# Cross-attention block: column-quartered matmuls gathered into one group in two steps

## The reference

```python
x = layer_norm(hidden_states, ln1_w, ln1_b)
q = (x @ q_w + q_b)          # 16 heads of 32
k = (ctx @ k_w + k_b); v = (ctx @ v_w + v_b)
attn = softmax(where(mask, q k^T * scale, min))
out = (attn @ v) @ cproj_w + cproj_b
hidden = out + hidden_states
y = gelu(layer_norm(hidden, ln2_w, ln2_b) @ fc_w + fc_b) @ proj_w + proj_b
return hidden + y
```

## Time and profile before

| | |
|---|---|
| median of 3 runs | 826.39 us (824.57 to 826.96) |
| the profiled execution | 823.19 us, span 821.4 us |
| TensorE matmuls busy | 788.1 us (96%) |
| VectorE busy | 449.1 us (55%) |
| GpSimd busy | 314.6 us (38%) |
| ScalarE busy | 276.6 us (34%) |

### The profile page before, as it was taken

How to read it: one execution, slowest core, us unless ns; L and a number is a source line. 1 busy time by engine, 2 the same in 40 slices (tenths; PEclk the granted TensorE clock), 3 DMA queues, 4 the chain that set the end, 5 groups by cost and what they waited for, 6 DMA issues and landing times.

```text
span 821.4 us, 9736 instructions
## 1 busy us (share of the span) xinstructions
PE 788.1 (96%) x3728; PEld 558.1 (68%) x3728; DVE 449.1 (55%) x711; ACT 276.6 (34%) x483; POOL 314.6 (38%) x190
## 2 busy tenths in 40 slices
PE   7899999999999998999898899999999999999998
PEld 5788888644445444544543688888888888888886
DVE  6853344787866897688789735633323332332122
ACT  4434241366654654467347101121112111111111
POOL 2724040166973875488648436432002110112000
PEclk9999999999999999999999999999999999999999
DMA  8476385836534533537331245004000400020001
GB/s 308 129 243 231 120 253 143 257 79 161 125 91 131 166 79 91 168 79 182 102 103 39 69 150 162 31 0 155 1 0 1 154 1 0 1 84 20 0 1 51
DMA packets 53102, 85.39 MB, mean 104 GB/s; under 512 B 5344, under 2 KB 13796, under 8 KB 53056
## 3 DMA queue, kind: packets, MB, share of 16 engines
q1 hardware_dynamic: 52912, 84.75, 34.8%
q10 hardware_dynamic: 144, 0.02, 0.0%
HBM read 59.45 MB, written 25.18 MB: 103 GB/s over the span
## 4 chain that ended last, share of the span: by engine, by line
PE 79%; DVE 14%; DMA 2%; issue 2%; ACT 1%; SPq 1%; POOL 0%; DVEq 0%; POOLq 0%
PE ps L383 20%; PE ps L384 20%; PE ps L385 20%; DVE mx L859 5%; PE ps L483 5%; PE ps L499 5%; PE ps L468 5%; PE ps L514 3%; DVE BIG L899 2%; DVE R L976 1%; PE ps L527 1%; DVE R L864 1%; DVE R L818 1%; DMA R<-in_k_w 1%; PE ps L442 1%
## 5 line engine op out<-in xcount | busy, mean ns | idle before, releaser
L1123 POOL TENSOR_TENSOR R<-Pt 128x1024 f32<-128x1024 f32 x59 | 144.1, 2460 | 127.3 <-PE ps L514 76.6
L859 DVE TENSOR_REDUCE mx<-ps 128x1 f32<-128x512 f32 x256 | 162.8, 680 | 40.7 <-PE ps L468 40.4
L692 ACT ACTIVATE Pt<-ps 128x512 f32<-128x512 f32 x256 | 135.0, 600 | 99.7 <-PE ps L483 96.5
L1012 DVE CAST HR<-R 128x512 fp32r<-128x512 f32 x52 | 24.2, 466 | 184.6 <-ACT R L726 184.6
L726 ACT ACTIVATE R<-ps,cols 128x512 f32<-128x512 f32 x52 | 35.9, 690 | 205.4 <-PE ps L385 205.4
L468 PE MATMUL ps<-BIG 97*128 97x512 f32 x256 | 94.6, 414 | 9.2 <-DVE mx L859 9.2
L483 PE MATMUL ps<-BIG 98*128 98x512 f32 x256 | 99.5, 433 | 3.6 <-ACT Pt L692 2.3
L483 PEld LDWEIGHTS ps<-BIG 98*128 98x128 f32 x256 | 43.9, 191 | 71.2 <-ACT Pt L692 36.8
L383 PE MATMUL ps<-BIG,HR 128*128 128x512 f32 x192 | 74.9, 390 | 2.7 <-DVE HR L1014 2.7
L383 PE MATMUL ps<-YT,BIG 128*128 128x512 f32 x192 | 75.8, 395 | 0.0
L385 PE MATMUL ps<-YT,BIG 128*128 128x512 f32 x192 | 74.8, 390 | 0.0
(11 more groups left out here) (107 smaller groups left out, 1298.0 us busy)
## 6 DMA issues: line engine op xcount, KB each, us to landing
BIG<-qs SPq DMA_DIRECT2D x48, 256.0 KB
BIG<-ks SPq DMA_DIRECT2D x48, 256.0 KB
ks<-BIG SPq DMA_DIRECT2D x32, 256.0 KB, 2.0
qs<-BIG SPq DMA_DIRECT2D x32, 256.0 KB, 5.5
R<-hd SPq DMA_DIRECT2D x28, 256.0 KB, 4.2
R<-in_x SPq DMA_DIRECT2D x16, 256.0 KB, 4.5
hd<-R SPq DMA_DIRECT2D x16, 256.0 KB, 2.0
RW<-in_fc_w SPq DMA_DIRECT2D x16, 256.0 KB, 2.8
```

The costliest lines, as they stand in the source:

```text
L692: eng.activation(Pt[:, r, j % 2, :], bank(3 + place % 3), ACT.Exp, scale=SCALE).then_inc(S["a_ra"], 1)
L859: eng.tensor_reduce(mx[:, s % 2, 4 * j + qc:4 * j + qc + 1], bank(place % 3), AX.X, ALU.max).then_inc(S["v_rb"], 1)
L1123: eng.tensor_tensor(R0[:, 2 * hp:2 * hp + 2, :], Pt[:, (r - 2) % 6, :, :], Pt[:, r, :, :], ALU.add).then_inc(S["g_ac"], 1)
```

## The change

The sums of a pair and the products of two steps now stand together, in one group in every second step: at an even step i, before `s2(i, 2)`, come the sums of steps i-4 and i-3, then `pv(i - 2)` and `pv(i - 1)`. The pair sums have a second place (half of RAWY to pair 17, then RW to pair 21; from there R0 alone again), so that GpSimd waits for an earlier sum. `divide_a` moves from m=1 to m=2 of its step. The first slabs' load also waits for the last sum that reads RW. In batch 0, the second x is turned behind the last Q projection, with ScalarE's and VectorE's parts of it.

```diff
+        SECOND = RW.rearrange("p a (h t) -> p (a h) t", h=2)
+        def pair(m):
+            if m % 2 == 0 or m > 21:
+                return R0[:, :, :]
+            return RAWY[:, 0] if m <= 17 else SECOND
+        def pair_before(m):
+            return m - 1 if m < 23 else m
...
                 if f < 2:
                     sp.wait_ge("p_pv", 48)
+                    sp.wait_ge("p_sm", 22)
...
-                    ins = eng.matmul(bank(7)[32 * j:32 * j + 32, :], ones[:, :], R0[:, j, :], start=kc == 1, stop=kc == 3)
+                    ins = eng.matmul(bank(7)[32 * j:32 * j + 32, :], ones[:, :], pair(i // 2)[:, j, :], start=kc == 1, stop=kc == 3)
...
+            def columns(i):
+                if i >= 4:
+                    sums((i - 4) // 4, (i - 4) % 4 + 1)
+                pv(i - 2)
+                pv(i - 1)
...
-                    if b == 0 and g == 1:
+                    if b == 0 and g == 3:
                         x_turn(1)
...
                 for m in range(4):
+                    if m == 2 and i >= 2 and i % 2 == 0:
+                        columns(i)
                     if m >= 2:
                         s2(i, m)
...
-                    if m == 2 and kc == 1 and i >= 5:
-                        sums(s - 1, 3)
...
-                if kc == 3:
-                    sums(s, 1)
-                if i >= 1:
-                    pv(i - 1)
...
-            pv(NI - 1)
+            columns(NI)
...
-                    if m == 1 and i >= 5 and kc == 2:
+                    if m == 2 and i >= 5 and kc == 2:
                         divide_a(s - 1)
...
-                    dve.wait_ge("p_sm", i // 2)
-                    eng.tensor_tensor(R0[:, 2:4, :], Pt[:, (r - 2) % 6, :, :], Pt[:, r, :, :], ALU.add).then_inc(S["v_ac"], 1)
+                    dve.wait_ge("p_sm", pair_before(i // 2))
+                    eng.tensor_tensor(pair(i // 2)[:, 2:4, :], Pt[:, (r - 2) % 6, :, :], Pt[:, r, :, :], ALU.add).then_inc(S["v_ac"], 1)
...
-                        else:
-                            pool.wait_ge("p_sm", i // 2)
-                        eng.tensor_tensor(R0[:, 2 * hp:2 * hp + 2, :], Pt[:, (r - 2) % 6, :, :], Pt[:, r, :, :],
+                        elif i >= 5:
+                            pool.wait_ge("p_sm", pair_before(i // 2))
+                        eng.tensor_tensor(pair(i // 2)[:, 2 * hp:2 * hp + 2, :], Pt[:, (r - 2) % 6, :, :], Pt[:, r, :, :],
```

## The result

The kernel with the change takes 862.3 us (median of 4, 858.46 to 863.76) against 826.16 us (4, 824.57 to 826.96) before: a ratio of 1.043, 95% interval 1.0395 to 1.047. It is slower, as forecast, but by 36 us and not by 12; the time lies 12 us above the end of the range. The profiled execution has a span of 860.7 us (before 821.4), with a mean granted clock of 0.968 (before 0.992): some 55 us of it at 1.2 GHz, against 13 before.

A forecast was written before the change was run, and what follows sets the result against it. It took TensorE (97% busy) as the bound, VectorE close behind and setting the new loops. Start +0.8, steps 4 to 20 +6.1, 20 to 36 +2.1, 36 to 52 +0.9, tail +1, turn +0.8: +11.7, so 838 us, range 823 to 850.

The forecast's parts named there:

- The two loops: Plain attention steps: loop without divides 7.0 us, with divides 9.1, or 9.7 with the wait for GpSimd.
- The lock: VectorE's last divide waits for GpSimd's pair add to end: 0.6 us, bounds 0 and 2.4, in eight loops.
- The start: Second x turned later in batch 0: TensorE's stall grows by 0.65 us; taken as +0.8, bounds -3 and +1.5.
- The fourth rival: TensorE's clock falls in the loops, a group costing up to 2.7 us more: 847 to 855 us; chance 0.11.
- the first: The rival in which the attention loops hold as worked out: slower, 829 to 845 us; chance 0.68.
- case 1: The likeliest outcome, attention loops as worked out and slower: 838 us; chance 0.68.
- ScalarE at nothing: Attention loops: the forecast's sum held no term for waits on ScalarE's exponentials.
- An even step's end at its own length: VectorE's work at an even step's end counts in full: 0.7 us a statistic, 0.6 the variances, 0.7 a turned y.
- The sum: Whole kernel: all terms together +11.7 us on the profiled execution's 823.19, giving 834.9, or 838 as median.

The follow-up runs named there:

- experiment 9: Changed kernel with three repeats of a first-pass matmul at m=2 of kc=3 and m=0 of kc=0, outside the projections' steps: 858.5 us, ratio 1.040.
- experiment 2: Changed kernel with VectorE's maxima reading 32 of 512 columns: 830.9 us, ratio 1.010 to the kernel before.
- experiment 4: Changed kernel with all three divides ahead of the maximum of m=2 at kc=2, where VectorE idles for the group: 835.4 us, ratio 1.014.
- Experiment 6: Kernel before with only the two places for the pair sums, no column group moved: 827.7 us, ratio 1.007.
- experiment 3: Changed kernel with one place for the pair sums, every pair in R0: 862.3 us, ratio 1.048 to the kernel before.
- experiment 8: Kernel before with the lone sums of kc=1 joined to that step's product, and the first divide ahead of the maximum of m=0 at kc=2: 824.7 us, ratio 1.003.

## Why the prediction was right in sign and short in size

**The two loops: right.** 7.24 for 7.0, and 9.61 for 9.7; VectorE's idle at a group 2.18 and 2.32 for 2.1. Four plain steps at full clock take 16.85 us, 1.5 more than before; experiment 9 held that at full clock (7.25 and 9.63), and experiments 2 and 4 show that it is the divides in VectorE's queue.

**The lock: right as a mechanism.** Experiment 6 shows it alone, experiment 3 its absence. The 0.6 us taken for a divide compare with 1.14 - 0.68 = 0.46 at the median. In two loops, at steps 31 (above) and 27, it was 2.2, inside the bounds; at twice 2.2 - 0.6 that is 3 us of the stretch from 20 to 36. The two divides that I had left out as held by an output projection, at steps 23 and 39, met an add as well and took 1.72 each. The Trainium skill's page "SBUF — State Buffer", section SBUF: two separate sides, calls this an exclusive lock, as cited in the prediction. The trace agrees: 2.87 us for a divide that begins with an add, 0.67 without.

**The start: right.** The stall grew by 0.74 us, for 0.65.

**The clock: the step that failed.** The fourth rival was priced by itself, with a chance of 0.11, and kept out of the likeliest sum. It does not exclude the first: the loops hold and the clock falls in them. The groups alone lost 13.5 us to it, 12.7 more than before (16 by the estimate that takes in ordinary matmuls), above the 9 to 11 that I had worked out, as it struck in eight groups and not four, three of them after a hole of ScalarE's and one behind holes of only 0.74 and 0.60. I had a row for it and took the hole before the last tile as some 1.3 us; it was 1.07. With the rival's 9 to 11 us added to case 1 the forecast would have been 847 to 849, still short of 862.

**ScalarE at nothing: wrong.** In the rows of step 8 the exponentials wait behind the split of a divided step and the copy of the products (195.68 to 197.45). Holes for exponentials grew from 2.3 to 9.1 us, 1.3 at steps 8, 24 and 56, 1.1 at 40, 0.65 where a turned y stands. They stay with VectorE free (9.5 in experiment 2). I had worked out what the ring of three banks does to VectorE and not asked the same of the ring that ScalarE empties. That the split and the copy make these holes is read from the rows; no run moved them.

**An even step's end at its own length: too little where it meets the lock.** The variances were charged 0.6 us. At step 31 a small operation of GpSimd's (L1076) also waits for them and holds its adds back to 312.62; the divide comes 0.03 us later and so waits for a whole one.

**The sum.** Predicted +11.7, measured +39.3 between spans: 14.2 of holes behind maxima, 6.8 behind exponentials, 12.7 of groups at 1.2 GHz; the rest, 5.6, I can't place by rows. Some 3 of it would be ordinary matmuls at 1.2 GHz, by the estimate above. The switches saved are in it with the other sign, against the delays too short to be listed. Whether steps 36 to 58 lose by VectorE's later adds or by the projections stays open: no run took those apart.

## What to carry to other kernels

When small blocks of one engine are gathered into a long one, compare its length with what each ring of buffers holds of the other engines' work, for every ring and not only the busiest, and put serial work of the waiting engine into the block's shadow: that alone gave back 24 to 27 of 36 us here. Where a block makes holes on TensorE, count the clock in the likeliest sum: behind holes of some 1 us a group took up to 2.6 us more here. Work taken off the busiest engine can show in plain stretches and not in the whole, as the switch saved in every four steps of experiment 8 did.

## What the runs showed of the hardware beyond what I expected

- The clock fell behind holes of 0.6 to 2.1 us beside a column-quartered group of 2.7 us, and the same pair of holes, 0.75 and 1.06, stood before groups of 2.71 us four times and before groups of 5.28 and 4.02. In the kernel before, a hole of 1.48 us at 395.03 was followed by matmuls at 2.4 GHz, and one of 1.62 at 402.73 by a projection's matmuls at 1.2 GHz, 0.63 us each where 0.39 is usual.
- Repeating three matmuls whose result was there already made a loop no longer and its group shorter, by up to 2.57 us.
- A divide of 0.67 us takes up to 2.89 when it begins with GpSimd's add of 2.4, and its median was highest, 1.80, with the pair sums in two places and the groups as before.
- With the maxima at 0.19 us the changed loops with divides still took 7.4 us and not the 6.8 worked out from TensorE's rows, and a mask load that had been hidden came to be waited for, up to 1.6 us at a time.
